# The odd text row's matmuls spread over four column groups, the halves added behind the transpose, and the mask rows copied by GpSimd

## What is computed

```python
h = jnp.tanh(txt_proj[:, None, :, :] + feat_proj[:, :, None, :] + b)   # 4 x 1024 x 77 x 256
rho = jnp.einsum('bftd,d->bft', h, w[:, 0])
rho = rho + (1.0 - qm)[:, None, :] * NEG
att = jax.nn.softmax(rho, axis=-1)
txt_h = jnp.einsum('bft,btd->bfd', att, textual_features)
w_s = jnp.tanh(txt_h @ Wcw.T + bcw); b_s = jnp.tanh(txt_h @ Wcb.T + bcb)
x = x + w_s * features + b_s          # features: the layer norm of x
```

## Time and profile before

| | |
|---|---|
| timed runs | 894.20, 891.44, 893.63 us |
| profiled execution | 891.94 us, of it 890.1 us span |
| TensorE busy (L786 of it) | 799.7 us (304.4 us) |
| ScalarE busy (tanh L994 of it) | 759.5 us (520.9 us) |
| VectorE busy (adds L1375 of it) | 714.6 us (417.9 us) |
| GpSimd busy | 308.1 us |

### The profile page before, as it was taken

How to read it: one execution, slowest core, us unless ns; L and a number is a source line. 1 busy time by engine, 2 the same in 40 slices (tenths; PEclk the granted TensorE clock), 3 DMA queues, 4 the chain that set the end, 5 groups by cost and what they waited for, 6 DMA issues and landing times.

```text
span 890.1 us, 14100 instructions
## 1 busy us (share of the span) xinstructions
PE 799.7 (90%) x5385; PEld 473.9 (53%) x5385; DVE 714.6 (80%) x1396; ACT 759.5 (85%) x589; POOL 308.1 (35%) x531
## 2 busy tenths in 40 slices
PE   6975679569998999989999999999988999999996
PEld 5321123124443444444444455555766999999986
DVE  5899888898889689997879996795887877676641
ACT  3989999999999999999998999997753677676672
POOL 3310540615543006775002650033403145555424
PEclk9899999999999999999999999999999999999999
DMA  8000000000001000200000010002202365544513
GB/s 261 25 1 0 1 1 1 1 24 1 25 1 48 1 1 25 71 1 2 24 1 1 24 49 1 24 1 97 71 24 78 105 174 142 143 106 126 138 19 41
DMA packets 32407, 41.82 MB, mean 47 GB/s; under 512 B 2366, under 2 KB 29012, under 8 KB 32340
## 3 DMA queue, kind: packets, MB, share of 16 engines
q1 hardware_dynamic: 26083, 32.49, 11.1%
q0 software_dynamic: 6144, 8.39, 5.8%
q10 hardware_dynamic: 112, 0.04, 0.0%
HBM read 28.33 MB, written 12.58 MB: 46 GB/s over the span
## 4 chain that ended last, share of the span: by engine, by line
PE 52%; ACT 20%; DVE 19%; issue 4%; POOL 3%; DMA 0%; POOLq 0%; DVEq 0%; ACTq 0%
ACT z L994 18%; PE bank L786 12%; DVE z L1375 11%; PE bank L913 10%; PE bank L936 9%; PE bank L843 7%; PE bank L828 6%; PE bank L762 2%; PE bank L714 1%; POOL xn L1139 1%; DVE att L1444 1%; PE bank L951 1%; ACT z L990 1%; PE bank L816 1%; PE bank L887 1%
## 5 line engine op out<-in xcount | busy, mean ns | idle before, releaser
L994 ACT ACTIVATE z<-z 128x4096 f32<-128x4096 f32 (+5 forms) x157 | 520.9, 3360 | 10.9 <-DVE z L1375 10.7
L1375 DVE TENSOR_SCALAR z<-feat,txt_bias 128x1024 f32<-128x1024 f32 (+1 forms) x722 | 417.9, 651 | 29.0 <-PE bank L786 28.1
L786 PE MATMUL bank<-z,window 128*32 128x512 f32 x2464 | 304.4, 604 | 63.0 <-ACT z L994 61.8
L786 PEld LDWEIGHTS bank<-z,window 128*32 128x32 f32 x2464 | 70.3, 110 | 247.8 <-issue 138.4
L843 PE MATMUL bank<-ws_sb,u 128*128 128x256 f32 x512 | 126.0, 387 | 1.5 <-ACT u L1043 1.5
L843 PEld LDWEIGHTS bank<-ws_sb,u 128*128 128x128 f32 x512 | 92.8, 190 | 35.5 <-issue 21.1
L828 PE MATMUL bank<-tr,ws_s 128*128 128x512 f32 x384 | 107.8, 417 | 2.8 <-issue 2.8
L1200 POOL TENSOR_TENSOR scale<-wb,x_ry 128x4 f32<-128x4 f32 x7 | 10.5, 1498 | 258.2 <-ACT wb L1005 258.2
L913 PE MATMUL bank<-xg_s,w_s 128*128 128x512 f32 x384 | 99.6, 397 | 0.2 <-DVE xg_s L1696 0.2
L936 PEld LDWEIGHTS bank<-w_s,hid_s 128*128 128x128 f32 x672 | 86.4, 188 | 4.0
L936 PE MATMUL bank<-w_s,hid_s 128*128 128x256 f32 x672 | 88.2, 280 | 0.0
(11 more groups left out here) (273 smaller groups left out, 780.1 us busy)
## 6 DMA issues: line engine op xcount, KB each, us to landing
w_raw<-in_L_ffn_W_dram SPq DMA_DIRECT2D x16, 1024.0 KB, 5.7
x_ring<-in_x_dram SPq DMA_DIRECT2D x8, 512.0 KB, 7.9
xn_dram<-xn SPq DMA_DIRECT2D x8, 512.0 KB, 2.9
out_dram<-x_ring SPq DMA_DIRECT2D x8, 512.0 KB, 3.0
u<-in_L_ffn_Ws_dram SPq DMA_DIRECT2D x1, 1024.0 KB, 11.5
ws_sb<-in_L_ffn_Ws_dram SPq DMA_DIRECT2D x1, 1024.0 KB, 14.2
xg<-xn_dram,idx POOLq DMA_INDIRECT x32, 4.4
out_dram<-y,idx POOLq DMA_INDIRECT x32, 3.9
```

Source lines behind the costliest of these rows:

```text
L786: ins = e.matmul(sums[v][32 * r:32 * r + 32, :], window[:, c, 31 - k:63 - k], z[:, n % ZB, at_piece:at_piece + TOK], start=(v, r) not in b ...
L994: e.activation(part, part, ACT.Tanh).then_inc(signal(*step), 1)
L1375: ins = e.tensor_scalar(z[:, n % ZB, i * width:(i + 1) * width], feat_of(units, c), bias_of(units, t, c), None, ALU.add)
```

## The change

The row t = 76 gets a place of its own. Its chunk c for unit v goes to group 2 (v mod 2) + c, row 0, and all other rows move by one (row k + 1). So the four matmuls of the last block of batches 0 to 2 lie in four groups, and the two of batch 3's lie in two. A unit's score of row 76 then stands in two halves in two groups, and `att_shift` adds them behind the transpose, in PSUM, into group 0 at row 20, which had held padding. The mask rows move accordingly, and their copy goes from VectorE's `reps` to a new step `mask_rows` on GpSimd. The number of matmuls and the order of the steps stay as they were.

```diff
-                                  [("reps",)], [("router_consts",), ("earlier",)]])
+                                  [("reps",), ("mask_rows",)], [("router_consts",), ("earlier",)]])
...
+    ODD = T - 1
...
+        def row_of(v, k, r, t, c):
+            return (C * (v % UPB) + c, 0) if t == ODD else (r, k + 1)
...
-                                    ins = e.matmul(sums[v][32 * r:32 * r + 32, :], window[:, c, 31 - k:63 - k],
+                                    g, at_row = row_of(v, k, r, t, c)
+                                    left[v, g] -= 1
+                                    ins = e.matmul(sums[v][32 * g:32 * g + 32, :], window[:, c, 31 - at_row:63 - at_row],
...
-                    e.wait_ge(*done("reps"))
+                    e.wait_ge(*done("mask_rows"))
...
@@ gpsimd @@
+                elif kind == "mask_rows":
+                    e.wait_ge(*done("wide_out", 0))
+                    e.wait_ge(consts, MASK_CLEAR)
+                    e.tensor_copy(mask_h[0:1, :, :, 1:I + 1], row[0:1, 0, :, :].rearrange("p b (i g) -> p b g i", g=G))
+                    for first in range(0, G, C):
+                        ins = e.tensor_copy(mask_h[0:1, :, first, 0], row[0:1, 0, :, ODD])
...
@@ vector @@
                 elif kind == "reps":
-                    e.wait_ge(consts, MASK_CLEAR)
...
-                    e.tensor_copy(mask_h[0:1, :, :, 0:I], row[0:1, 0, :, :].rearrange("p b (i g) -> p b g i", g=G)).then_inc(signal(*step), 1)
...
                 elif kind == "att_shift":
-                    link(e.tensor_reduce(biggest, rt[:, :, :, 0:I], AX.XY, ALU.max))
+                    g = C * (v % UPB)
+                    link(e.tensor_reduce(rt[:, :, 0, I], rt[:, :, g:g + C, 0], AX.X, ALU.add))
+                    e.wait_ge(vector_link, linked)
+                    link(e.tensor_reduce(biggest, rt[:, :, :, 1:I + 1], AX.XY, ALU.max))
                     e.wait_ge(vector_link, linked)
-                    e.tensor_tensor(a.rearrange("p j (g i) -> p j g i", g=G), rt[:, :, :, 0:I],
+                    e.tensor_tensor(a.rearrange("p j (g i) -> p j g i", g=G), rt[:, :, :, 1:I + 1],
```

More of the change, by code:

```diff
@@ L389, in xattn_moe_kernel @@
     assert D % P == 0 and CAP == TOK and I <= 32 and NT % JT == 0 and NH == 2 and UNITS % 2 == 0 and P % E == 0
+    assert T % G == 1 and G == UPB * C and I < 32
     assert CANDIDATES == BY_DVE + BY_ACT and NTOK % (2 * JT) == 0
@@ L701, in _ @@
             sums, begun = {}, set()
-            left = {(v, r): sum(p[0] == r for units, _, pieces in blocks if v in units for p in pieces)
-                    for v in range(UNITS) for r in range(G)}
+            left = {(v, g): sum(row_of(v, k, *p)[0] == g for units, k, pieces in blocks if v in units for p in pieces)
+                    for v in range(UNITS) for g in range(G)}
             def take(bank):
@@ L784, in _ @@
                                     at_piece = i * width + h * TOK
-                                    left[v, r] -= 1
-                                    ins = e.matmul(sums[v][32 * r:32 * r + 32, :], window[:, c, 31 - k:63 - k],
-                                                   z[:, n % ZB, at_piece:at_piece + TOK], start=(v, r) not in begun,
-                                                   stop=left[v, r] == 0)
-                                    begun.add((v, r))
+                                    g, at_row = row_of(v, k, r, t, c)
+                                    left[v, g] -= 1
+                                    ins = e.matmul(sums[v][32 * g:32 * g + 32, :], window[:, c, 31 - at_row:63 - at_row],
+                                                   z[:, n % ZB, at_piece:at_piece + TOK], start=(v, g) not in begun,
+                                                   stop=left[v, g] == 0)
+                                    begun.add((v, g))
                     ins.then_inc(signal(*step), 1)
@@ L1252, in _ @@
                                     ALU.subtract).then_inc(signal(*step), 1)
+                elif kind == "mask_rows":
[4 more added lines that the diff above has]
+                        ins = e.tensor_copy(mask_h[0:1, :, first, 0], row[0:1, 0, :, ODD])
+                    ins.then_inc(signal(*step), 1)
                 elif kind == "gather":
@@ L1399, in _ @@
                     e.wait_ge(*done("wide_out", 1))
-                    e.wait_ge(consts, MASK_CLEAR)
                     for i, rep in enumerate((cw_rep[:, :, 0, :], cw_rep[:, :, 1, :])):
-                        e.tensor_copy(rep.rearrange("p b (g i) -> p b g i", g=G),
-                                      row[:, 1 + i, :, :].rearrange("p b (i g) -> p b g i", g=G))
-                    e.tensor_copy(mask_h[0:1, :, :, 0:I], row[0:1, 0, :, :].rearrange("p b (i g) -> p b g i", g=G)).then_inc(signal(*step), 1)
+                        ins = e.tensor_copy(rep.rearrange("p b (g i) -> p b g i", g=G),
+                                            row[:, 1 + i, :, :].rearrange("p b (i g) -> p b g i", g=G))
+                    ins.then_inc(signal(*step), 1)
                 elif kind == "router_consts":
```

## The result

| | before | changed |
|---|---|---|
| timed runs, median | 893.63 us (891.44 to 894.20) | 887.89 us (887.30 to 888.52) |
| profiled execution, its span | 891.94, 890.1 us | 887.30, 885.5 us |
| TensorE busy, granted clock | 799.7 us, 0.993 | 798.3 us, 0.983 |
| L786, now L793 | 304.4 us, 604 ns | 301.4 us, 614 ns |

The ratio of the times is 0.9943, with a 95% interval from 0.9927 to 0.9960: faster, and 0.4 us from the forecast of 887.5.

The account below looks back on a forecast made before the run. ScalarE, TensorE and VectorE fill the tanh loop; savings count only where ScalarE idles. 2.33 + 2.58 + 0.95 + 0.25 = 6.1 us takes the profile from 891.94 to 885.8, the 893.63 median to 887.5; range 885.0 to 892.2 us.

Parts of the forecast that it names:

- batch 0: Behind batch 0: no gain in either direction, since VectorE waits there for ScalarE's exponential.
- batch 1: Behind batch 1: TensorE 2.58 us earlier, less 0.04 and 0.21 us for the sums, 2.33 us reaching ScalarE.
- batch 2: Behind batch 2: the full 2.58 us gained, against 2.75 us of idleness on ScalarE.
- end: End of batch 3, before the last `rho_out`: 1.00 us comes through, less 0.05 for the sum, 0.95 us taken.
- mask rows: Mask copy moved from VectorE to GpSimd: 0.33 us off the chain, less 0.08 for disturbed adds, gain 0.25 us.
- The odd block: Last block of batches 0 to 2 on TensorE: eight records take 2 steps instead of 8, 2.58 us less.
- The groups take turns: Rival on odd blocks: writes into two banks exclude each other, TensorE saves nothing, 893.7 us; chance 0.07.
- each change of group drains the array: Rival on odd blocks: records wait for each other's end, 4.83 us instead of 3.55, 896.7 us in all; chance 0.04.
- ScalarE absorbs it: Rival behind batches 1 and 2: other lateness fills ScalarE's idle rows, only 1.2 us left, 892.4 us; chance 0.14.
- the step on the sums: Batch 2 on VectorE: both added sums, 0.42 us, fall into its wait of 0.86 us.
- The cap of 1.00 us: Last `rho_out`: TensorE 1.7 us earlier, but VectorE's reciprocal ends at 616.16 us regardless, so 1.00 us comes through.
- TensorE's busy time: TensorE in L786's records: busy time falls by some 9 us, 9.5 at most.

Follow-up runs that it names:

- the repeat: The changed kernel profiled and timed once more, with nothing altered; median 888.48 us, 0.9953 of the kernel before.
- halves: Changed kernel with row 76's two halves in groups 0 and 1 for both units of a batch, two groups instead of four; 890.17 us, 0.9961 of before.
- no_sum: Changed kernel without the added sums, so the second half of row 76's score is left out; 886.89 us, 0.9939 of before.
- all_one: Changed kernel with the odd row's matmuls in one group again for all units, GpSimd's copies and added sums kept; 892.66 us, 0.9994 of before.
- mask16: Changed kernel with the large mask copy on GpSimd done sixteen times in a row; span 896.0 us against 884.0 us for the repeat.
- b3: Changed kernel with the odd row spread in batch 3 alone, the other batches in one group; 892.43 us, 0.9998 of before.
- sum5_six: Changed kernel with the added sum done five times in unit 6 alone; last `rho_turn` at 614.02 us instead of the repeat's 611.77 us.

## Why the prediction was right, and where it was off

| term | predicted gain | measured |
|---|---|---|
| batch 0 | 0 | 0.0 |
| batch 1 | 2.33 | 2.34 (26.21 - 23.87) |
| batch 2 | 2.58 | 2.34 (27.36 - 25.02) |
| end | 0.95 | 0.95 (17.37 - 16.42) |
| mask rows | 0.25 | 0.34 (the second set of adds starts at 51.41, was 51.75; ScalarE's tanh behind it 0.30 sooner, 65.97 for 66.27) |
| sum | 6.1 | 6.0; between the spans 6.1 (890.1 - 884.0, the repeat) |

- **The odd block.** Two steps, 1.07 us in all three batches, also with four groups writing to two banks. "The groups take turns" and "each change of group drains the array" are out, and with `halves` the rule has a third point: 8, 4 and 2 steps take 3.62, 1.91 and 1.07 us. The rule of the Trainium skill's page "TensorE: Matmul & The Clock Gate", Part 3, would have made batch 1 some 0.9 us poorer; the measured 2.34 us leaves no room for it.
- **Batch 1 and batch 0.** Right in mechanism and size. The lead went from TensorE's wait at `rho_out` to ScalarE's idle rows, and "ScalarE absorbs it" is refuted: 2.55 us gross come through. One sign missed: ScalarE's idle rows were to shrink to under 0.5 us behind each batch, and 0.57 and 0.94 us are left (0.56 and 0.85 in the repeat).
- **Batch 2: the step on the sums failed.** I let both sums disappear in VectorE's wait of 0.86 us. That wait did shrink to 0.64, but it ends with a release by TensorE that itself came less early than the odd block: from the block's start to these adds it is 11.58 us now (456.09 to 467.67) and was 13.92 (457.59 to 471.51), 2.34 us less, not 2.58. One sum of 0.20 us stays on the path, as `no_sum` confirms (24.82 against 25.02). A wait at the end of a loop through the other engines is no store of free time: what delays VectorE ahead of it also delays what it waits for.
- **The end.** Right in mechanism, and in size by luck. The added sum costs 0.14 us, not 0.05: it isn't beside TensorE's queue only (17.51 for `all_one`, 17.37 before). The cap of 1.00 us was 1.08, so the errors cancel.
- **The mask rows.** The whole length of the copy came back, and nothing was lost. But the ground was wrong: from four adds that lost 0.24 us beside a norm on GpSimd I took it that GpSimd hardly disturbs VectorE. The 0.24 was itself misread, a timeline's 2.89 us against a chain's 2.65; in the timeline four adds take 2.74, so it is 0.15. In that pair GpSimd was the one held up: its four pieces take 4.64 us there and 2.18 us at 599.37 us. In `mask16` it goes the other way, at 7.4 us for 15 copies more. That the change pays nothing is luck of its place in time.
- **TensorE's busy time: a miss.** I expected 9 us less of L786's records, and the profile after shows 3.0 less of them and 1.4 less in all. It is time at the granted clock, which was 0.983 instead of 0.993, and 1% of 800 us is 8 us. The repeat had 0.989, and TensorE's busy time fell to 792.9 us, L793's to 297.7, 6.9 and 6.7 less than before; the 0.4% that its clock still lacks are 3.2 us, which makes 10, an estimate. The failed step is that the clock was taken as unchanged, and its fall isn't all chance: in eight of the nine traces in which batch 0's odd block is shortened it is granted at half for 7 to 10 us between 134 and 188 us, and of the five others only in `b3`'s. ScalarE loses nothing by it there (23.43 against 23.41 us above).
- **The absolute time.** The changed kernel's profile was at 887.3 us, not 885.8. It had the stretch at half clock at 398 us, and the kernel before's had not; without it the repeat's span is 884.0 us, 6.1 below. So that the median came within 0.4 us of the forecast is partly luck. The forecast stood on the median of three executions, 893.63 us, where the later ones of the same kernel have 892.5; from there it would have been 886.4. And the changed kernel's medians, 887.89 and 888.48 us, lie above what its trace without the half clock shows (885.84): by medians the gain is 5.7 and 4.0 us, by the stages 6.0.

## What to carry to other kernels

Look for records that stand one behind the other in one column group while others idle; their price is a step each. Follow it to the engine that waits last: here the 2.55 us came through in full behind batches 1 and 2, and nothing in batch 0, where the wait was for another engine. Compare stages inside one trace, from an event ahead of the edit to one behind it: this told 0.2 us apart, where the medians of 4 to 12 executions could not tell 1. Compare the granted clock by stretch too before a difference of spans is read: in `mask16` 1.6 of 8.8 us had been there before the edit ran.

## What was not expected of the hardware

- A GpSimd instruction on 4 values a partition took 4.5 us, and 10.8 us in `sum5_six`, beside 35 adds of VectorE without a gap; behind the adds the next one took 0.20 us.
- Copies of one partition on GpSimd (0.76 us each in the changed kernel), sixteen in a row, slow four adds of 128 partitions beside them: 4.84 instead of 2.73 us.
- TensorE's clock was granted at half for 398.0 to 401.4 us in one execution of a program and at full in another; 1.6 us of the whole kernel.
